# Gate and up weights of a feed-forward unpacked in the feed-forward itself, down weights alone in the rotary stage

## The chip, the cores and the metric

The kernel runs on one core of one Trainium2 chip. The metric is the device time of one execution in microseconds (us). The engines are TensorE (PE; its weight loads are PEld), VectorE (DVE), ScalarE (ACT), GpSimd (POOL) and SyncE (SP), which only issues DMAs here. Each engine runs its own queue in order; semaphores are the only thing that ties the queues together.

## What is computed

Two transformer-like layers over 16 batches of 64 tokens with 512 channels (1024 tokens). Layer 0 is a windowed attention and a base layer with routed low-rank experts. Layer 1 is an attention with 32 query heads, 8 key heads and rotary embedding, then a feed-forward with 4-bit weights (inner width 1376). Only the last matters for the change:

```python
def _dequant(qweight, scales, qzeros, g_idx):
    shifts = jnp.arange(PACK, dtype=jnp.uint32) * BITS            # 8 values of 4 bits in one word
    w = (qw[:, None, :] >> shifts[None, :, None] & MAXQ).reshape(-1, qweight.shape[1])
    z = ((qz[:, :, None] >> shifts[None, None, :] & MAXQ) + 1).reshape(qzeros.shape[0], -1)
    s = scales[g_idx]
    return (w.astype(scales.dtype) - z[g_idx].astype(scales.dtype)) * s
...
Wg = _dequant(gate_qweight, ...)   # 512 x 1376
Wu = _dequant(up_qweight, ...)     # 512 x 1376
Wd = _dequant(down_qweight, ...)   # 1376 x 512
# feed-forward: (silu(x @ Wg) * (x @ Wu)) @ Wd
```

Unpacking an element is thus shift and mask, minus zero point, times scale; zero point and scale are rows of a table chosen by `g_idx`.

## The kernel before

The program is a sequence of stages: `windowed_attention`, `routed_lora`, `rotary_attention`, `gate_up`, `down`. Between two stages all engines meet at a barrier. Matrix products are made by `three_passes` (L754 to L756): each float32 operand is split into a high part (by ScalarE) and a low part (high subtracted, by GpSimd for weights, by VectorE for activations), and high x high, low x high and high x low are summed.

`rotary_attention` handles the eight key heads in four pairs of two. A pair has 16 steps, a step being one tile of 128 tokens of one key head with its four query heads. In all there are 64 steps, numbered `n = step_number(b, c)` from 0. Every engine has its own function `step(b, c)`, written out by hand, and the order of its lines is the order of its queue; work of neighbouring tiles is interleaved in it. With j = n mod 4:

- TensorE: `turn` of tile n-2, `project` of one rotary unit, `project_out` of tile n-3 (L754 to L756 with `woh`/`wol` and `oh`/`ol`), `weighted` of n-2, a second `project`, the value projection if j = 2, `scores` of n+1 (L1578). `project_out` waits for `ol_ready`, from VectorE's `low_out`.
- VectorE: `low_out` of tile n-3 (L1465), `minimum` of n (L1444, L1449), `subtract_zeros` (L877), `rotary` (L1433 to L1435) for the first unit, `add` of n-3 (L1470), `probabilities` (L1455, L1459), `multiply_scales` (L886), `rotary` for the second unit, `unpack_weights` of the next unit of weights (L867). Rotary units are 0 and 1 in steps with j = 0, 2 and 3 with j = 1, 4 with j = 2, none with j = 3 (`ROTARY_OF`).
- GpSimd: `rotary_sum` for the same units (L1297, L1301), `low_piece` (L214) of a piece of the next head's projection weights when one is due (n mod 8 from 1 to 6, `PIECE_AT`; the key and value pieces are 128 x 512, the others 128 x 1024), then `gather_scales` (L858), an indirect DMA that brings scale and zero-point rows.
- SyncE: `load_piece` (L198), which waits in this same step for the `low_piece` whose buffer it reuses, `load_packed` (L850), `store_weights` (L899).

The 4-bit weights are unpacked in 43 of the 64 steps, one unit a step: `Q_UNITS` = 43 units, 32 of them "wide" (128 x 344 of gate or up) and 11 of "down" (128 x 512). Unit u is worked on in step u+1 and its rows are gathered two steps earlier into one of two buffers `sz`. The finished float32 weights are stored in HBM (`w_wide`, `w_down`).

`gate_up` first normalises the activations (`norm_rows`, `norm_turn`, `norm_high`, `norm_low`), then makes 11 tiles of the inner width. For each it loads one gate and one up tile of weights (`wf`, L1714, four buffers, two issues a tile pair), ScalarE makes `wh` (L1737), GpSimd `wl` (L1727), TensorE four products, ScalarE the tanh (L1749), and VectorE two operations for each half of the tokens (L1773, L1775). `down` multiplies by the down weights `wd`, which `gate_up` loads whole at its beginning.

Of the kernel before, what the change touches and what calls it, by code (L numbers as in the profile page):

```python
# [86 lines left out]
def build_program(nc, a, out):  # L87
    with ExitStack() as top:
# [24 lines left out]
        g["w_wide"] = nc.dram_tensor("w_wide", (2 * DC * P, INTER), F32).ap()  # L113
        g["w_down"] = nc.dram_tensor("w_down", (INTER, D), F32).ap()
        g["w_stored"] = [top.enter_context(nc.semaphore(f"w_stored{i}")) for i in range(2)]
# [714 lines left out]
def unit_shape(u):  # L830

    if u < WIDE_UNITS:
        return P, QCOLS
    return inner(u - WIDE_UNITS), D

def load_packed(sp, a, g, u):

    rows, cols = unit_shape(u)
    packed = P // PACK  # L840
    if u >= 2:
        sp.wait_ge(g["q_used"], u - 1)
    if u < WIDE_UNITS:
        chunk, q = u // QPIECES, u % QPIECES
        w = a[MATS[chunk // DC][0] + "_qweight"]
        src = bass.AP(w.tensor, w.offset + packed * (chunk % DC) * INTER + QCOLS * q, [[INTER, packed], [0, PACK], [1, cols]])
    else:
        w = a["down_qweight"]
        src = bass.AP(w.tensor, w.offset + packed * (u - WIDE_UNITS) * D, [[D, rows // PACK], [0, PACK], [1, cols]])
    sp.dma_start(g["qraw"][0:rows, u % 2, 0:cols], src).then_inc(g["q_landed"][u % 2], 16)  # L850

def gather_scales(pool, g, u):

    if u >= 2:
        pool.wait_ge(g["w_ready"], u - 1)
    table, width = (g["table_wide"], 2 * QCOLS) if u < WIDE_UNITS else (g["table_down"], 2 * D)
    pool.indirect_dma_start(g["sz"][:, u % 2, 0:width], None, table,  # L858
                            bass.IndirectOffsetOnAxis(ap=g["index"][:, u:u + 1], axis=0)).then_inc(g["sz_landed"][u % 2], 16)

def unpack_weights(dve, g, u):

    rows, cols = unit_shape(u)
    raw = g["qraw"][0:rows, u % 2, 0:cols]
    dve.wait_ge(g["q_landed"][u % 2], 16 * (u // 2 + 1))
    dve.tensor_scalar(raw, raw, g["nib"][0:rows, 0:1], 15, ALU.logical_shift_right, ALU.bitwise_and).then_inc(g["qn_ready"], 1)  # L867

def subtract_zeros(dve, g, u):  # L870

    rows, cols = unit_shape(u)
    dve.wait_ge(g["qn_ready"], u + 1)
    dve.wait_ge(g["sz_landed"][u % 2], 16 * (u // 2 + 1))
    if u >= 2:
        dve.wait_ge(g["w_stored"][u % 2], 16 * (u // 2))
    dve.tensor_tensor(g["dq"][0:rows, u % 2, 0:cols], g["qraw"][0:rows, u % 2, 0:cols], g["sz"][0:rows, u % 2, cols:2 * cols],  # L877
                      ALU.subtract).then_inc(g["q_used"], 1)

def multiply_scales(dve, g, u):

    rows, cols = unit_shape(u)
    w = g["dq"][0:rows, u % 2, 0:cols]
    dve.wait_ge(g["q_used"], u + 1)
    dve.tensor_tensor(w, w, g["sz"][0:rows, u % 2, 0:cols], ALU.mult).then_inc(g["w_ready"], 1)  # L886

def store_weights(sp, g, u):

    rows, cols = unit_shape(u)
    if u < WIDE_UNITS:
        chunk, q = u // QPIECES, u % QPIECES
        dst = g["w_wide"][chunk * P:chunk * P + rows, q * QCOLS:(q + 1) * QCOLS]
    else:
        r0 = (u - WIDE_UNITS) * P
        dst = g["w_down"][r0:r0 + rows, :]
    sp.wait_ge(g["w_ready"], u + 1)
    sp.dma_start(dst, g["dq"][0:rows, u % 2, 0:cols]).then_inc(g["w_stored"][u % 2], 16)  # L899
# [237 lines left out]
def rotary_attention(nc, a, g):  # L1137
# [37 lines left out]
    def unit_at(n):  # L1175

        return n - 1 if 1 <= n <= Q_UNITS else None
# [787 lines left out]
```

## Time and profile before

| | before |
|---|---|
| median of 3 timed runs | 1169.86 us (1169.71 to 1169.95) |
| the profiled execution's own time | 1171.48 us |
| its span in the profile | 1169.7 us |
| busy: PE, DVE, POOL, ACT | 1037.1, 796.0, 457.7, 349.8 us |
| rotary stage, first to last masked scores (L1444) | 363.5 to 951.8 us |
| start of the first load of `gate_up` | 976.0 us |

The span runs from the first to the last instruction that the profile shows. Every row of the trace gives start, duration, engine, line, operation and tiles; an idle time ahead of an instruction stands in brackets with the engine and line that ended it. L numbers are lines of the kernel before.

### The profile page before, as it was taken

The numbers are of one execution on the slowest core, as the hardware profiler recorded it, in microseconds if no ns is written. First come the engines' busy times: TensorE is split into PE (matmuls) and PEld (weight loads), VectorE is DVE, ScalarE is ACT, GpSimd is POOL, SyncE is SP.
The fourth block names the chain that finished last, engine by engine and source line by source line (L and its number), as shares of the span: only waits on it lengthen the run. The fifth ranks groups of instructions, "written<-read, shape, count | busy, mean of one in ns | idle before, by whom it ended". The sixth has DMA issues, their size and how long they took to land. (4 is left out here: it accounts for less than half of the span.)

```text
span 1169.7 us, 13349 instructions
## 1 busy us (share of the span) xinstructions
PE 1037.1 (89%) x4696; PEld 741.4 (63%) x4696; DVE 796.0 (68%) x1251; ACT 349.8 (30%) x926; POOL 457.7 (39%) x296
## 2 busy tenths in 40 slices
PE   5688877877878799999999999999999986999998
PEld 2333333344557567777777677677777765888787
DVE  4899998759566687778878888787676655222223
ACT  3232332213212332333333333333343332222131
POOL 3566655445515443444434434434243102222121
PEclk8899998869888899999999999999999998999999
DMA  7000000000311332332333325421010005211001
GB/s 258 1 1 0 1 1 1 1 18 1 104 50 52 118 123 78 127 112 88 109 100 118 126 80 168 161 97 45 27 46 18 1 2 168 53 38 32 1 1 72
DMA packets 60962, 75.91 MB, mean 65 GB/s; under 512 B 8444, under 2 KB 44068, under 8 KB 60888
## 3 DMA queue, kind: packets, MB, share of 16 engines
q1 hardware_dynamic: 56032, 57.66, 15.7%
q0 software_dynamic: 4144, 17.04, 4.5%
q8 instruction: 38, 0.62, 0.2%
q10 hardware_dynamic: 720, 0.36, 0.1%
q14 instruction: 28, 0.23, 0.1%
HBM read 64.37 MB, written 10.68 MB: 64 GB/s over the span
## 5 line engine op out<-in xcount | busy, mean ns | idle before, releaser
L1301 POOL TENSOR_TENSOR shared<-shared 128x512 f32<-128x512 f32 x64 | 83.7, 1307 | 201.6 <-DVE shared L1435 201.3
L754 PE MATMUL ps<-woh,oh 128*128 128x512 f32 x256 | 108.8, 425 | 32.9 <-DVE ol L1465 28.1
L1370 ACT ACTIVATE c_xn<-c_xn,c_mn 128x64 f32<-128x64 f32 x256 | 86.0, 337 | 155.6 <-DVE c_mn L1449 155.6
L754 PE MATMUL ps<-xh,wqh 128*128 128x512 f32 x256 | 106.6, 416 | 0.4 <-DVE shared L1435 0.4
L756 PE MATMUL ps<-woh,ol 128*128 128x512 f32 x256 | 104.7, 409 | 0.0
L755 PE MATMUL ps<-wol,oh 128*128 128x512 f32 x256 | 104.3, 408 | 0.0
L1433 DVE TENSOR_TENSOR shared<-ps,cs 128x512 f32<-128x512 f32 x80 | 54.9, 687 | 70.6 <-PE ps L756 70.6
L756 PE MATMUL ps<-xh,wql 128*128 128x512 f32 x256 | 100.4, 392 | 0.0
L755 PE MATMUL ps<-xl,wqh 128*128 128x512 f32 x256 | 99.9, 390 | 0.0
L540 DVE TENSOR_TENSOR r<-ps,vpad 128x512 f32<-128x512 f32 x128 | 79.4, 683 | 27.4 <-PE ps L629 27.4
L372 POOL TENSOR_TENSOR r<-r 128x1024 f32<-128x1024 f32 x32 | 77.1, 2410 | 50.4 <-DVE r L540 50.3
L1470 DVE SCALAR_TENSOR_TENSOR x<-ps,gate,x 128x512 f32<-128x512 f32 x64 | 48.0, 750 | 70.9 <-PE ps L756 70.2
L754 PEld LDWEIGHTS ps<-woh,oh 128*128 128x128 f32 x256 | 50.1, 196 | 54.1 <-DVE ol L1465 31.8
L1578 PEld LDWEIGHTS ps<-shared 128*128 128x128 f32 x512 | 66.3, 193 | 8.7 <-issue 5.2
L1383 ACT ACTIVATE oh<-ps 128x512 fp32r<-128x512 f32 x64 | 38.3, 598 | 104.8 <-PE ps L1603 104.8
L754 PE MATMUL ps<-xh,wh 128*128 128x512 f32 (+1 forms) x176 | 68.7, 390 | 1.0 <-POOL wl L1727 1.0
L1578 PE MATMUL ps<-shared 128*128 128x64 f32 x512 | 65.2, 271 | 3.8 <-POOL shared L1301 3.8
L756 PE MATMUL ps<-xh,wl 128*128 128x512 f32 (+1 forms) x176 | 68.6, 390 | 0.0
L755 PE MATMUL ps<-xl,wh 128*128 128x512 f32 (+1 forms) x176 | 68.5, 389 | 0.0
L1727 POOL TENSOR_TENSOR wl<-wf,wh 128x512 fp32r<-128x512 f32 (+1 forms) x22 | 28.6, 1318 | 82.9 <-ACT wh L1737 82.9
L629 PE MATMUL ps<-turned,spread 128*128 128x512 f32 x128 | 54.2, 506 | 7.4 <-DVE r L540 5.9
L754 PEld LDWEIGHTS ps<-xh,wqh 128*128 128x128 f32 x256 | 48.1, 188 | 18.2 <-issue 8.6
(172 smaller groups left out, 2387.8 us busy)
## 6 DMA issues: line engine op xcount, KB each, us to landing
stage<-in_wq SPq DMA_DIRECT2D x16, 512.0 KB, 4.1
stage<-in_wo SPq DMA_DIRECT2D x16, 512.0 KB, 3.8
w_wide<-dq SPq DMA_DIRECT2D x32, 172.0 KB, 4.9
wf<-w_wide SPq DMA_DIRECT2D x20, 256.0 KB, 3.4
qraw<-in_gate_qweight SPq DMA_DIRECT2D x16, 172.0 KB, 4.3
qraw<-in_up_qweight SPq DMA_DIRECT2D x16, 172.0 KB, 3.7
qraw<-in_down_qweight SPq DMA_DIRECT2D x10, 256.0 KB, 4.5
w_down<-dq SPq DMA_DIRECT2D x10, 256.0 KB, 6.0
```

The source lines that it names most:

```text
L372: pool.tensor_tensor(r2[:, 2 * m:2 * m + 2, :], r[:, w:w + 2, :], r[:, w + GW:w + GW + 2, :], ALU.add).then_inc(rsum_ready, 1)
L540: dve.tensor_tensor(r[:, w, :], RING[(2 + n) % 3], vpad[:, i % 3, w:w + D], ALU.mult)\
L629: pe.matmul(RING[(2 + n) % 3], spread[:, w % GW, :], turned[:, w // GW, :], start=True, stop=True)\
L754: pe.matmul(dst, lh, rh, start=(first and c == 0), stop=False)
L755: pe.matmul(dst, lh, rl, start=False, stop=False)
L756: last = pe.matmul(dst, ll, rh, start=False, stop=(final and c == chunks - 1))
L1301: pool.tensor_tensor(qT[:, h * TPH:(h + 1) * TPH, :, p - 1, :], turn(ra), turn(rb), ALU.add)\
L1370: act.activation(part, part, ACT.Exp, scale=-1.0, bias=mn[:, c % 2, u:u + 1], accum_out=sm[:, c % 2, u:u + 1]).then_inc(exp_ready, 1)
L1383: act.activation(by_batch(oh, c), weighted_sum, ACT.Copy).then_inc(oh_ready, 1)
L1433: dve.tensor_tensor(A, bank, cs[:, 0, :].unsqueeze(1).broadcast_to([P, nb, C]), ALU.mult)
L1470: dve.scalar_tensor_tensor(x[:, i, :], ps[:, WO[c % 2], :], gate[:, 1:2], x[:, i, :], ALU.mult, ALU.add)\
L1578: last = pe.matmul(dst[:, u * C:(u + 1) * C], qT[:, i, k, 2 * hp:2 * hp + 2, :].rearrange("p h t -> p (h t)"), kT[:, i * P + k * C:i * P + ...
```

## The change

Gate and up units are no longer unpacked in the rotary stage. There, for each of their 32 units, GpSimd gathers the scale and zero rows as before, and SyncE copies them from the buffer into a new tensor `sz_wide` in HBM. The 11 down units are still unpacked on VectorE, in steps with n mod 4 = 2 (n = 2, 6, ... 42). The wide fetches fill the other steps, from n = 3 to 44. `PLAN` maps a step to its fetch; a fetch is issued by GpSimd in the step before (`ahead`), and waits for the store (wide) or the multiplication (down) of the fetch two earlier, whose buffer it takes. `gate_up` now loads the packed words (four DMAs a tile) and the scale and zero rows (two DMAs) into three buffers, and VectorE unpacks each tile with three operations of 128 x 512, twice within the normalisation, twice behind it, then two tiles ahead of use.

```diff
+DOWN_AT = 2
+def fetch_plan():
+    plan, wide, down, n = {}, 0, 0, 2
+    while wide < WIDE_UNITS or down < NTI:
+        if n % TPH == DOWN_AT and down < NTI:
+            plan[n] = (len(plan), WIDE_UNITS + down)
+            down += 1
+        elif n % TPH != DOWN_AT and wide < WIDE_UNITS:
+            plan[n] = (len(plan), wide)
+            wide += 1
+        n += 1
+    return plan
+def fetch_done(eng, g, f):
+    u = next(unit for number, unit in PLAN.values() if number == f)
     if u < WIDE_UNITS:
...
+        same = [v for number, v in PLAN.values() if number <= f and number % 2 == f % 2 and v < WIDE_UNITS]
+        eng.wait_ge(g["sz_stored"][f % 2], 16 * len(same))
     else:
...
+        eng.wait_ge(g["wd_ready"], u - WIDE_UNITS + 1)
+def fetch_scales(pool, g, f, u):
+    if f >= 2:
+        fetch_done(pool, g, f - 2)
+    table = g["table_wide"] if u < WIDE_UNITS else g["table_down"]
+    pool.indirect_dma_start(g["sz"][:, f % 2, 0:width_of(u)], None, table,
+                            bass.IndirectOffsetOnAxis(ap=g["index"][:, u:u + 1], axis=0)).then_inc(g["sz_landed"][f % 2], 16)
+def store_scales(sp, g, f, u):
+    chunk, q = u // QPIECES, u % QPIECES
+    sp.wait_ge(g["sz_landed"][f % 2], 16 * (f // 2 + 1))
+    sp.dma_start(g["sz_wide"][chunk * P:(chunk + 1) * P, :, q * QCOLS:(q + 1) * QCOLS],
+                 g["sz"][:, f % 2, 0:2 * QCOLS].rearrange("p (e n) -> p e n", e=2)).then_inc(g["sz_stored"][f % 2], 16)
...
@@ SyncE, step @@
-                u = unit_at(n)
-                if u is not None:
-                    if 2 <= u + 2 < Q_UNITS:
-                        load_packed(sp, a, g, u + 2)
-                    store_weights(sp, g, u)
+                if n - 1 in PLAN:
+                    f, u = PLAN[n - 1]
+                    if u < WIDE_UNITS:
+                        store_scales(sp, g, f, u)
+                    else:
+                        store_down(sp, g, u - WIDE_UNITS)
+                if n in PLAN and WIDE_UNITS <= PLAN[n][1] < Q_UNITS - 2:
+                    load_down(sp, a, g, PLAN[n][1] - WIDE_UNITS + 2)
...
@@ GpSimd, step @@
-                u = unit_at(step_number(b, c))
-                if u is not None and u + 2 < Q_UNITS:
-                    gather_scales(pool, g, u + 2)
+                ahead = step_number(b, c) + 1
+                if ahead in PLAN:
+                    fetch_scales(pool, g, *PLAN[ahead])
...
@@ VectorE, step @@
-                u = unit_at(step_number(b, c))
-                if u is not None:
-                    subtract_zeros(dve, g, u)
+                f, u = PLAN.get(step_number(b, c), (0, 0))
+                t = u - WIDE_UNITS
+                if t >= 0:
+                    subtract_zeros(dve, g, f, t)
...
@@ gate_up @@
+        DEQUANT_AT = {3: 0, 5: 1}
...
+                if k >= 3:
+                    sp.wait_ge(w_ready, k - 2)
+                for c in range(DC):
+                    src = bass.AP(q.tensor, q.offset + packed * c * INTER + P * t, [[INTER, packed], [0, PACK], [1, w]])
+                    sp.dma_start(raw[:, k % 3, c * P:c * P + w], src).then_inc(landed[k % 3], 16)
+                rows = g["sz_wide"][m * DC * P:(m + 1) * DC * P, :, t * P:t * P + w].rearrange("(c p) e n -> p e c n", p=P)
+                for e in range(2):
+                    sp.dma_start(columns(sz[:, k % 3, e, :], k), rows[:, e, :, :]).then_inc(landed[k % 3], 16)
+                if k == 5:
...
+            for i in range(2, NT):
+                norm_rows(dve, g, n, xn, i)
+                norm_low(dve, g, n, XT, i - 2)
+                if i in DEQUANT_AT:
+                    dequantise(DEQUANT_AT[i])
+            norm_low(dve, g, n, XT, NT - 2)
+            norm_low(dve, g, n, XT, NT - 1)
+            dequantise(2)
+            dequantise(3)
             for t in range(NTI):
...
+                if t + 2 < NTI:
+                    unpack(2 * t + 4)
+                    subtract(2 * t + 4)
+                    unpack(2 * t + 5)
+                    scale(2 * t + 4)
+                    subtract(2 * t + 5)
+                    scale(2 * t + 5)
```

Three queues show what moved. GpSimd in steps 5 and 6: `shared` are the rotary sums, `wol` the split of an output piece, the DMA the gather. Before:

```order
L1301 TENSOR_TENSOR shared<-shared 128x8x64 [waits c_sc_done,c_rope_a] x2
L214 TENSOR_TENSOR wol<-stage,woh 128x1024 [waits high_ready]
L858 DMA sz<-table_wide,index 128x688 [waits c_w_ready]
L1301 TENSOR_TENSOR shared<-shared 128x8x64 [waits c_sc_done,c_rope_a]
L214 TENSOR_TENSOR wol<-stage,woh 128x1024 [waits high_ready]
```

and after the change:

```order
L1328 TENSOR_TENSOR shared<-shared 128x8x64 [waits c_sc_done,c_rope_a] x2
L215 TENSOR_TENSOR wol<-stage,woh 128x1024 [waits high_ready]
L876 DMA sz<-table_down,index 128x1024 [waits sz_stored0]
L1328 TENSOR_TENSOR shared<-shared 128x8x64 [waits c_sc_done,c_rope_a]
L215 TENSOR_TENSOR wol<-stage,woh 128x1024 [waits high_ready]
```

The gather stands in the same place behind the split. Before it fetched for step 7 and waited for VectorE's multiplication; now it fetches the down rows for step 6 and waits for a store.

SyncE in the same two steps (the first three rows are step 5, the others step 6), before:

```order
L198 DMA stage<-in_wk 128x4x128 [waits low_ready]
L850 DMA qraw<-in_gate_qweight 128x1x344 [waits c_q_used]
L899 DMA w_wide<-dq 128x344 [waits c_w_ready]
L198 DMA stage<-in_wq 128x4x256 [waits low_ready]
L850 DMA qraw<-in_gate_qweight 128x1x344 [waits c_q_used]
L899 DMA w_wide<-dq 128x344 [waits c_w_ready]
```

and after (the first two rows are step 5):

```order
L199 DMA stage<-in_wk 128x4x128 [waits low_ready]
L884 DMA sz_wide<-sz 256x1x344 [waits c_sz_landed0]
L199 DMA stage<-in_wq 128x4x256 [waits low_ready]
L884 DMA sz_wide<-sz 256x1x344 [waits c_sz_landed1]
L895 DMA qraw<-in_down_qweight 128x1x512 [waits c_q_used]
```

The store that signals `sz_stored0` stands behind the load of a weight piece, which waits for `low_ready`, the split of GpSimd's step 5.

VectorE at the beginning of step 6, after the change:

```order
L1490 TENSOR_TENSOR ol<-ps,oh 128x2x4x64 [waits c_oh_ready]
L1469 SCALAR_TENSOR_TENSOR c_xn<-ps,mask 128x256 [waits c_pr_ready,c_sc_done]
L1474 TENSOR_REDUCE c_mn<-c_xn 128x4 [waits c_masked]
L912 TENSOR_TENSOR dq<-qraw,sz 128x512 [waits w_stored0,c_sz_landed0,c_qn_ready]
L1458 TENSOR_TENSOR shared<-ps,cs 128x512 [waits c_rope_ready,c_proj_done]
```

The subtraction (L912, before L877) waits for the landing of that gather, and the rest of the step is queued behind it.

## Rows read from the trace of the kernel before

**Rows 1.** Page, busy time, share of the span and instructions
```profile
PE 1037.1 (89%) x4696; PEld 741.4 (63%) x4696; DVE 796.0 (68%) x1251; ACT 349.8 (30%) x926; POOL 457.7 (39%) x296
```

**Rows 2.** Timeline of DVE: masked scores of steps 4, 44, 48, 56
```profile
399.95 0.41 DVE L1444 SCALAR_TENSOR_TENSOR c_xn<-ps,mask 128x256 f32<-128x256 f32 x1
...
793.78 0.41 DVE L1444 SCALAR_TENSOR_TENSOR c_xn<-ps,mask 128x256 f32<-128x256 f32 x1
...
827.71 0.42 DVE L1444 SCALAR_TENSOR_TENSOR c_xn<-ps,mask 128x256 f32<-128x256 f32 x1
...
899.26 0.42 DVE L1444 SCALAR_TENSOR_TENSOR c_xn<-ps,mask 128x256 f32<-128x256 f32 x1
```

**Rows 3.** Timelines of POOL, steps 21 and 22, and of DVE
```profile
578.56 2.52 POOL L214 TENSOR_TENSOR wol<-stage,woh 128x1024 fp32r<-128x1024 f32 x1
581.21 1.08 POOL L858 DMA_INDIRECT sz<-table_wide,index  x1
...
580.10 1.35 DVE L877 TENSOR_TENSOR dq<-qraw,sz 128x344 f32<-128x344 int32 x1
```

**Rows 4.** Timelines of POOL, DVE and PE, steps 49 to 51, without unpacking
```profile
849.50 1.30 POOL L1301 TENSOR_TENSOR shared<-shared 128x512 f32<-128x512 f32 x1 [5.13 <-DVE shared L1435]
850.75 1.31 POOL L214 TENSOR_TENSOR wkvl<-stage,wkvh 128x512 fp32r<-128x512 f32 x1
...
850.50 0.42 DVE L1449 TENSOR_REDUCE c_mn<-c_xn 128x4 f32<-128x256 f32 x1
...
858.33 0.48 PE L754 MATMUL ps<-woh,oh 128*128 128x512 f32 x1
```

**Rows 5.** DMA issues, KB, us to landing: 785:790, 792:800, 765:772, 738:746
```profile
w_down<-dq SPq DMA_DIRECT2D x1, 256.0 KB, 3.3
...
w_down<-dq SPq DMA_DIRECT2D x1, 192.0 KB, 4.0
...
sz<-table_down,index POOLq DMA_INDIRECT x1, 4.2
...
w_down<-dq SPq DMA_DIRECT2D x2, 256.0 KB, 6.6
...
sz<-table_down,index POOLq DMA_INDIRECT x2, 7.0
```

**Rows 6.** Timeline of DVE, step 42: a down unit, to the end of `low_out`
```profile
778.49 0.72 DVE L877 TENSOR_TENSOR dq<-qraw,sz 128x512 f32<-128x512 int32 x1
...
782.79 2.92 DVE L886 TENSOR_TENSOR dq<-dq,sz 128x512 f32<-128x512 f32 x1
785.63 0.47 DVE L867 TENSOR_SCALAR qraw<-qraw,nib 96x512 int32<-96x512 int32 x1
786.02 0.68 DVE L1465 TENSOR_TENSOR ol<-ps,oh 128x512 fp32r<-128x512 f32 x1
```

**Rows 7.** PE after its longest gap; then windows, with PEclk before the last two
```profile
391.91 0.77 PE L754 MATMUL ps<-woh,oh 128*128 128x512 f32 x1 [6.08 <-DVE ol L1465]
...
396.00:398.00 2.00, 2.00 (x8) 1.06 (x6) 0.59 (x1) 0.00 (x0) 1.45 (x1) 0.52 0.00 0
398.00:400.00 2.00, 2.00 (x19) 1.75 (x16) 1.97 (x7) 1.20 (x3) 0.60 (x1) 1.00 0.54 169
```

**Rows 8.** Timelines of POOL and DVE: gather behind step 1's split, step 2's subtraction
```profile
384.95 0.97 POOL L858 DMA_INDIRECT sz<-table_wide,index  x1
...
382.81 0.82 DVE L877 TENSOR_TENSOR dq<-qraw,sz 128x344 f32<-128x344 int32 x1
```

**Rows 9.** `gate_up`: timelines of PE and DVE; DMA issues of 975:1030
```profile
984.36 0.47 PE L754 MATMUL ps<-xh,wh 128*128 128x512 f32 x1 [0.99 <-POOL wl L1727]
...
999.40 0.69 DVE L1773 SCALAR_TENSOR_TENSOR sg<-th,ps 128x512 f32<-128x512 f32 x1 [2.59 <-ACT th L1749]
...
1010.28 0.69 DVE L1773 SCALAR_TENSOR_TENSOR sg<-th,ps 128x512 f32<-128x512 f32 x1 [2.59 <-ACT th L1749]
...
wf<-w_wide SPq DMA_DIRECT2D x14, 256.0 KB, 3.7
```

More of the change, by code:

```diff
@@ L112, in build_program @@
         g["table_down"] = nc.dram_tensor("table_down", (GD, 2 * D), F32).ap()
-        g["w_wide"] = nc.dram_tensor("w_wide", (2 * DC * P, INTER), F32).ap()
+        g["sz_wide"] = nc.dram_tensor("sz_wide", (2 * DC * P, 2, INTER), F32).ap()
         g["w_down"] = nc.dram_tensor("w_down", (INTER, D), F32).ap()
+        g["sz_stored"] = [top.enter_context(nc.semaphore(f"sz_stored{i}")) for i in range(2)]
         g["w_stored"] = [top.enter_context(nc.semaphore(f"w_stored{i}")) for i in range(2)]
@@ L853, in gather_scales @@
[L853 to L867, printed above, removed]
@@ L870, in subtract_zeros @@
[L870 to L886, printed above, removed]
@@ new lines, with rows_of, width_of @@
+PLAN = fetch_plan()
+def rows_of(u):
+    return P if u < WIDE_UNITS else inner(u - WIDE_UNITS)
+def width_of(u):
+    return 2 * QCOLS if u < WIDE_UNITS else 2 * D
+def fetch_done(eng, g, f):
+    u = next(unit for number, unit in PLAN.values() if number == f)
+    if u < WIDE_UNITS:
+        same = [v for number, v in PLAN.values() if number <= f and number % 2 == f % 2 and v < WIDE_UNITS]
+        eng.wait_ge(g["sz_stored"][f % 2], 16 * len(same))
+    else:
+        eng.wait_ge(g["wd_ready"], u - WIDE_UNITS + 1)
@@ new lines, in load_down, with unpack_down @@
+def load_down(sp, a, g, t):
+    rows = inner(t)
+    if t >= 2:
+        sp.wait_ge(g["q_used"], t - 1)
+    w = a["down_qweight"]
+    src = bass.AP(w.tensor, w.offset + P // PACK * t * D, [[D, rows // PACK], [0, PACK], [1, D]])
+    sp.dma_start(g["qraw"][0:rows, t % 2, :], src).then_inc(g["q_landed"][t % 2], 16)
+def unpack_down(dve, g, t):
+    raw = g["qraw"][0:inner(t), t % 2, :]
+    dve.wait_ge(g["q_landed"][t % 2], 16 * (t // 2 + 1))
+    dve.tensor_scalar(raw, raw, g["nib"][0:inner(t), 0:1], 15, ALU.logical_shift_right, ALU.bitwise_and).then_inc(g["qn_ready"], 1)
@@ new lines, in subtract_zeros, with multiply_scales @@
+def subtract_zeros(dve, g, f, t):
+    w = inner(t)
+    dve.wait_ge(g["qn_ready"], t + 1)
+    dve.wait_ge(g["sz_landed"][f % 2], 16 * (f // 2 + 1))
+    if t >= 2:
+        dve.wait_ge(g["w_stored"][t % 2], 16 * (t // 2))
+    dve.tensor_tensor(g["dq"][0:w, t % 2, :], g["qraw"][0:w, t % 2, :], g["sz"][0:w, f % 2, D:2 * D], ALU.subtract)\
+       .then_inc(g["q_used"], 1)
+def multiply_scales(dve, g, f, t):
+    w = g["dq"][0:inner(t), t % 2, :]
+    dve.wait_ge(g["q_used"], t + 1)
+    dve.tensor_tensor(w, w, g["sz"][0:inner(t), f % 2, 0:D], ALU.mult).then_inc(g["wd_ready"], 1)
@@ L903, in routed_lora, with store_down @@
+def store_down(sp, g, t):
+    rows = inner(t)
+    sp.wait_ge(g["wd_ready"], t + 1)
+    sp.dma_start(g["w_down"][t * P:t * P + rows, :], g["dq"][0:rows, t % 2, :]).then_inc(g["w_stored"][t % 2], 16)
 def routed_lora(nc, a, g):
@@ L1200, in rotary_attention @@
         g["dq"] = sb("dq", [P, 2, D])
-        for name in ("qn_ready", "q_used", "w_ready"):
+        for name in ("qn_ready", "q_used", "wd_ready"):
             g[name] = sem(name)
@@ L1495, in step @@
                     probabilities(b, c)
-                if u is not None:
-                    multiply_scales(dve, g, u)
+                if t >= 0:
+                    multiply_scales(dve, g, f, t)
                 for p in units[1:]:
                     rotary(b, sl + 1, p)
-                if u is not None and u + 1 < Q_UNITS:
-                    unpack_weights(dve, g, u + 1)
+                if 0 <= t < NTI - 1:
+                    unpack_down(dve, g, t + 1)
             norm_rows(dve, g, n, xn, 0)
@@ L1514, in _ @@
                 rotary(0, 0, p)
-            unpack_weights(dve, g, 0)
+            unpack_down(dve, g, 0)
             for c in range(HEAD):
@@ L1684, in gate_up @@
         step = sem("step")
-        wf_landed = [sem(f"wf_landed{i}") for i in range(4)]
+        landed = [sem(f"landed{i}") for i in range(3)]
+        qn_ready = sem("qn_ready")
+        q_used = sem("q_used")
+        w_ready = sem("w_ready")
         wd_landed = sem("wd_landed")
```

78 lines of the change are left out of this document (36 added, 42 removed).

## The prediction, made before the changed kernel ran

> **What bounds the kernel now.** The page comes first: TensorE is busy for 89% of the span, more than any other engine [rows 1]. The change touches two stages, so the next view is the timeline, read by step of the rotary stage. A step n (0 to 63) is one pass of `step` on each engine; on VectorE it begins with the masked scores, L1444. Step 4 begins at 399.95 us and step 44 at 793.78: 393.83 us for forty steps, each with one unit of weights to unpack. Steps 48 to 56 have no unit and take 899.26 - 827.71 = 71.55 us for eight [rows 2]. In them TensorE has no gap. I call this the free rate. Forty steps at the free rate are 5 x 71.55 = 357.75 us, so all unpacking in this stretch costs 36.1 us today. It costs that much because VectorE does it between two things that TensorE waits for: `unpack_weights` stands ahead of `low_out`, whose result `project_out` needs.
>
> **What the change removes.** 32 of the 43 steps lose their three VectorE instructions. Taking the whole stretch at the free rate first, and pricing the steps that keep a down unit apart, removes 36.1 us.
>
> **What it adds in the rotary stage: a gather that is asked for too late.** Before, the gather for step n is issued in GpSimd's step n-2. Now it is issued as the last thing of GpSimd's step n-1. For a down unit n-1 is a step with two rotary sums, and the second of them needs the last VectorE work of that step. Before, in step 21, GpSimd's split of the weight piece runs from 578.56 to 581.08 and the gather behind it is issued at 581.21; VectorE's subtraction of step 22 begins at 580.10 [rows 3]. The gather that today serves a later step would, in the changed order, be the one this subtraction waits for. So it is late even if nothing else is.
>
> There is something else. The gather for step n first waits until the buffer two fetches back has been stored (`sz_stored0`). SyncE issues that store in its own step n-1, behind `load_piece`, and that load waits for the weight split of GpSimd's step n-1. So the chain is: last rotary sum, weight split, store issued and landed, gather issued and landed, subtraction. Nothing in it can overlap.
>
> I lay this chain over a free step (49 to 50), where no unpacking disturbs the times [rows 4]. The rotary sum runs 849.50 to 850.80. The split follows it: 1.31 us for the small piece (ends 852.06), 2.52 us for a large one [rows 3] (ends 853.3). Steps n with n mod 8 = 2 follow a small piece, those with n mod 8 = 6 a large one.
> - Store. Issue follows the split by about 0.1 us, behind the load's own 0.45. The nearest rows are a 256 KB store behind a 256 KB load, 3.3 us, and a 192 KB store behind a 512 KB load, 4.0 us [rows 5]. The new store has 344 KB, so I add 0.4 us to each, and 0.5 us more to the second, whose row was issued later behind its load. Behind a small load (large piece, n mod 8 = 6): 0.55 + 3.7 = 4.2 after the split, 857.5. Behind a large load (n mod 8 = 2): 0.55 + 4.9 = 5.4, also 857.5.
> - Gather. Alone on the queues, a down gather lands 4.2 us after its issue [rows 5]: 857.6 + 4.2 = 861.8, say 861.9.
> - VectorE then needs, from the subtraction to the end of `low_out`, 8.2 us: in step 42 it is 778.49 to 786.70, with the multiplication stretched to 2.92 us beside GpSimd's split, which follows in the same way here [rows 6]. So 870.1.
> - TensorE wants that result at 858.33 [rows 4]. It waits 11.8 us.
>
> **The clock.** After such a wait TensorE also restarts slowly. There is one gap of this kind in the stage already: 6.08 us before 391.91. The granted clock is 0.52 from 396 to 398 and 1.00 only from 398 [rows 7]: 6.1 us at 1.2 GHz instead of 2.4, so 3.0 us lost. A gap of 11.8 us is longer, and I charge 3.0 for each. The Trainium skill (TensorE: Matmul & The Clock Gate, Part 1) says that for modelling, the ramp penalty is under 1% of a typical kernel span. By that the clock term would be at most 11.7 us in all and the time 1273. The row here shows the loss after a single gap, and this kernel would have one per down unit.
>
> So each late unit costs 11.8 + 3.0 = 14.8 us. Ten of them (n = 6, 10, ... 42) cost 148.
>
> The eleventh, n = 2, has no store to wait for. The gather issued at that place before goes out at 384.95 [rows 8], about 2 us behind the start of the subtraction. With some 5 us to landing, VectorE resumes about 7 us later than today. The step before it loses 1.8 us of unpacking, and the clock is low there already. I take +5.
>
> For the transfers the Trainium skill (DMA: Bandwidth & Descriptors, Anatomy of one DMA) has a fixed 2.0 us plus the bytes at 436 GB/s. Estimated from that page, the store behind its load lands after 3.4 or 4.0 us and the gather after 3.2. The two stand on average 2 us below the chain above, which makes the sum about 20 us less, 1271. The rows of this trace are higher and are what I use.
>
> **What it adds in the feed-forward.** A pair of weight tiles lasts 10.88 us on TensorE (1010.28 - 999.40) [rows 9]. VectorE gains per pair two unpackings (0.47), two subtractions (0.72) and two multiplications (about the same when not beside GpSimd) [rows 6]: 3.8 us beside the four of 0.69 it has [rows 9], 6.6 of 10.88. If GpSimd's two subtractions of 1.3 us block it in full it is 9.2, still under. The weights are made two tiles ahead, so this hides. Loads: three times 256 KB a tile instead of one, each landing in 3.7 us [rows 9] and now in six issues. Two tiles every 10.88 us leave 5.4 for each, and a load with three times the packets should land in about 6 with three buffers in turn. It hides too; if it did not, it would cost 1 us a tile, 20 in all. What does not hide is the start. Today the first product begins at 984.36 [rows 9]. Now VectorE must wait in the middle of the normalisation for the six loads of tile 0 (last issue about 978.5, landed about 982) and put two sets of three operations (1.9 us each) ahead of the last rows. I count 3.7 us for the first and 1.9 for the second; about 5 us of it reaches TensorE.
>
> **Sum.** The span before is 1169.7 us, as is the median of the timed runs (1169.86), so I add to that. 1169.7 - 36.1 + 148 + 5 + 5 = 1291.6.
>
> **The rivals.**
> - Not slower: the gather is in time after all. If GpSimd runs far enough ahead of VectorE, the data lie there when the subtraction comes. Then a down unit costs only what VectorE's 8.2 us exceed the room: 850.9 + 8.2 - 858.3 = 0.8 us, eleven times, so 1169.7 - 36.1 + 9 + 5 = 1148. It decides at the landing: the gather may land up to about 850.9 in the clock of [rows 4]. Against it: the sum ahead of the gather needs VectorE's own rotary work and itself ends at 850.80. It could only hold if the wait order were another than the code has. Chance 0.03.
> - The store is not on the path (it lands while the split runs). Then only the gather's own lead counts: 853.3 or 852.1, plus 0.1 + 4.2, plus 8.2, against 858.3, on average 6.9 us, with the clock 9.9. Ten times is 99: 1242. For it speaks only that buffers alternate; against it, that the store stands behind a load that waits for the split. Chance 0.07.
> - The clock costs nothing, as it falls rarely: 1262. Chance 0.05.
> - The chain is dearer, since the transfers meet others: in a busy stretch the same store takes 6.6 and the gather 7.0 us [rows 5]. Most of that traffic is gone, but GpSimd's other gathers now wait for stores too, and could push its rotary sums, on which the scores depend. At 5 us more a unit: 1341. Half of it is as likely as the whole. Chance 0.11.
>
> **How the numbers follow.** The forecast has 0.74. Within it VectorE's part may be 2.2 us shorter (the multiplication takes 0.72 instead of 2.92 if it misses GpSimd's split), and store and gather together 1 us shorter or 2.5 longer (half of the busy stretch's surplus): 1260 to 1317. The range must reach towards the cheaper rivals and the dearer one: 1242 to 1335. A measurement of this kernel can tell about 0.2% from no change. Faster by more than that is the first rival, 0.03; within it 0.01, for a half-late gather that uses up the gain; slower 0.96.
>
> **What would show it.** In the profile after: ten gaps of about 12 us ahead of `project_out` in the steps after a down unit, put down to VectorE's `ol`; VectorE idle about 11 us ahead of the down subtraction, released by the landing of `sz<-table_down`; GpSimd idle ahead of the down gather, released by a store into `sz_wide`; low granted clock after each gap; 71.5 us per eight steps plus two stalls, so about 101. In the feed-forward the first product comes some 5 us later after the stage's start and a pair still takes 10.9 us. The prediction is wrong if the down gather is issued before the last rotary sum of its step, if the gaps are under 8 us, or if pairs in the feed-forward take over 11.5 us.

## The result, and the profile after

| | before | after |
|---|---|---|
| median of the timed runs | 1169.78 us (4 runs) | 1287.70 us (4 runs, 1286.35 to 1290.57) |
| ratio to before | | 1.101 (95% interval 1.099 to 1.103) |
| span of the profiled execution | 1169.7 us | 1285.7 us |
| mean granted clock of TensorE | 0.946 | 0.906 |

The changed kernel is 118 us slower; 1291.6 was forecast. The spans can be cut at the same events in both traces (a step begins with its masked scores, now L1469):

| stretch | before | after | difference | forecast |
|---|---|---|---|---|
| start to step 0 | 363.52 | 363.24 | -0.3 | 0 |
| steps 0 to 4 (the eleventh unit, n = 2) | 36.43 | 40.48 | +4.05 | +5 |
| steps 4 to 44 (ten down units) | 393.83 | 496.16 | +102.3 | +111.9 |
| steps 44 to 63 | 157.98 | 159.16 | +1.2 | 0 |
| step 63 to the start of `gate_up` | 24.20 | 24.22 | 0 | 0 |
| `gate_up` and `down` | 193.71 | 202.44 | +8.7 | +5 |

The page of after, busy times first, which answers to [rows 1]; then its costliest idle times (line, engine, out<-in, count | busy, mean ns | idle before, releaser):

```profile
PE 1047.8 (81%) x4696; PEld 752.9 (59%) x4696; DVE 772.8 (60%) x1221; ACT 350.9 (27%) x926; POOL 456.9 (36%) x296
...
L755 PE MATMUL ps<-woh,oh 128*128 128x512 f32 x256 | 113.3, 443 | 131.1 <-DVE ol L1490 74.2
...
L912 DVE TENSOR_TENSOR dq<-qraw,sz 128x512 f32<-128x512 int32 (+1 forms) x11 | 7.6, 692 | 117.6 <-DMA sz<-table_down,index 117.6
```

TensorE and VectorE do nearly the work of before, and both have more idle time. The two large idle times stand where the chain of the prediction puts them: ahead of the down subtraction (L912), ended by the landing of its gather, and ahead of `project_out`, ended by `low_out` (L1490). The second is more than half of the 131.1 us; the rest is put down to "issue", and stands in the same places.

The third wait of the chain is in the view of waits for the stretch 403 to 900 us (steps 4 to 44: waiting engine, tile and line, what ended it, us in total, times, longest):

```profile
POOL sz L876 <- DMA sz_wide<-sz: 126.1, 25, 5.8
...
DVE dq L912 <- DMA sz<-table_down,index: 110.2, 10, 11.7
```

GpSimd's 25 waits there are for fetches of both kinds. The ten ahead of a down gather last 4.1 to 5.7 us, 5.0 on average.

One unit from start to end, n = 26. Timelines of POOL, DVE and PE (start, us, engine, line, operation, idle time before in brackets):

```profile
671.85 1.29 POOL L1328 TENSOR_TENSOR shared<-shared 128x512 f32<-128x512 f32 x1 [5.13 <-DVE shared L1460]
673.10 1.30 POOL L215 TENSOR_TENSOR wkvl<-stage,wkvh 128x512 fp32r<-128x512 f32 x1
680.00 0.96 POOL L876 DMA_INDIRECT sz<-table_down,index  x1 [5.60 <-DMA sz_wide<-sz]
...
684.40 0.69 DVE L912 TENSOR_TENSOR dq<-qraw,sz 128x512 f32<-128x512 int32 x1 [11.12 <-DMA sz<-table_down,index]
688.65 2.82 DVE L920 TENSOR_TENSOR dq<-dq,sz 128x512 f32<-128x512 f32 x1
691.79 0.68 DVE L1490 TENSOR_TENSOR ol<-ps,oh 128x512 fp32r<-128x512 f32 x1
...
692.57 0.77 PE L755 MATMUL ps<-woh,oh 128*128 128x512 f32 x1 [11.63 <-issue]
...
693.98 0.63 PE L755 MATMUL ps<-woh,oh 128*128 128x512 f32 x1
694.41 0.63 PE L756 MATMUL ps<-wol,oh 128*128 128x512 f32 x1
```

and the two DMAs that SyncE issued behind that split (672 to 676 us; count, KB each, us to landing):

```profile
stage<-in_wq SPq DMA_DIRECT2D x1, 512.0 KB, 4.3
sz_wide<-sz SPq DMA_DIRECT2D x1, 344.0 KB, 4.9
```

Read it as a chain: the last rotary sum, the split, which ends at 674.40, the store behind the load (4.9 us), the gather at 680.00, landed 4.3 us later, the subtraction at 684.40, `low_out` at 691.79, TensorE at 692.57. Laid against [rows 4], each piece is there and they follow one another. The trace writes "issue" instead of VectorE for this gap, but it ends as `low_out` does.

Behind the gap the products follow each other every 0.43 us (693.98 to 694.41) instead of about 0.23. The windows of the same place (engines' busy time with counts, then PEclk, DMA share, GB/s) answer to [rows 7]:

```profile
690.00:692.00 2.00, 0.00 (x0) 0.00 (x0) 2.00 (x3) 0.00 (x0) 0.92 (x1) 0.50 0.00 1
694.00:696.00 2.00, 2.00 (x6) 1.61 (x5) 0.00 (x0) 1.67 (x6) 0.71 (x1) 0.50 0.51 167
696.00:698.00 2.00, 2.00 (x7) 1.06 (x6) 0.00 (x0) 0.00 (x0) 1.98 (x2) 0.51 0.44 135
698.00:700.00 2.00, 2.00 (x18) 1.67 (x18) 1.90 (x4) 1.17 (x2) 1.63 (x2) 1.00 0.25 70
```

TensorE had stood idle since 680.9. It is granted 1.2 GHz (0.50) in the last part of this gap and on to about 698, then 2.4 GHz.

### The profile page after: what moved, and what is told of

Read it like the earlier page. It is cut to its first block and busy times, and to the rows that moved or that the text cites. A ratio compares the mean times of both kernels' runs of the same rounds, so it can differ in the third digit from the quotient of the medians.

```text
span 1285.7 us, 13384 instructions
## 1 busy us (share of the span) xinstructions
PE 1047.8 (81%) x4696; PEld 752.9 (59%) x4696; DVE 772.8 (60%) x1221; ACT 350.9 (27%) x926; POOL 456.9 (36%) x296
## 5 line engine op out<-in xcount | busy, mean ns | idle before, releaser
L755 PE MATMUL ps<-woh,oh 128*128 128x512 f32 x256 | 113.3, 443 | 131.1 <-DVE ol L1490 74.2
L755 PEld LDWEIGHTS ps<-woh,oh 128*128 128x128 f32 x256 | 53.3, 208 | 146.9 <-issue 69.4
L756 PE MATMUL ps<-wol,oh 128*128 128x512 f32 x256 | 109.4, 427 | 0.0
L757 PE MATMUL ps<-woh,ol 128*128 128x512 f32 x256 | 109.2, 427 | 0.0
L541 DVE TENSOR_TENSOR r<-ps,vpad 128x512 f32<-128x512 f32 x128 | 79.4, 683 | 28.6 <-PE ps L630 28.6
L912 DVE TENSOR_TENSOR dq<-qraw,sz 128x512 f32<-128x512 int32 (+1 forms) x11 | 7.6, 692 | 117.6 <-DMA sz<-table_down,index 117.6
L1771 POOL TENSOR_TENSOR wl<-wf,wh 128x512 fp32r<-128x512 f32 (+1 forms) x22 | 31.6, 1453 | 88.6 <-ACT wh L1781 88.6
L757 PEld LDWEIGHTS ps<-woh,ol 128*128 128x128 f32 x256 | 53.5, 209 | 13.8
```

What stands on the lines that cost most here:

```text
L541: dve.tensor_tensor(r[:, w, :], RING[(2 + n) % 3], vpad[:, i % 3, w:w + D], ALU.mult)\
L755: pe.matmul(dst, lh, rh, start=(first and c == 0), stop=False)
L756: pe.matmul(dst, lh, rl, start=False, stop=False)
L757: last = pe.matmul(dst, ll, rh, start=False, stop=(final and c == chunks - 1))
L1771: pool.tensor_tensor(tile_view(wl, k), tile_view(wf, k), tile_view(wh, k).bitcast(F32), ALU.subtract)\
```

## The experiments

The traces show that the chain exists. They don't show that its parts cost what the table gives them: that the store's place behind a load matters, that the relief is 36 us once the chain is gone, and that the slow clock costs anything. Each of the following kernels takes one of these. Before ran beside them at 1168.48 us (e1 to e4) and 1168.88 us (e5 to e7).

### e1: the store ahead of the load

```diff
@@ SyncE, step @@
-                due = piece_due(c, last)
-                if due:
-                    piece, db, odd = due
-                    load_number(PIECES * (2 * (b + db) + odd) + piece + 2)
                 if n - 1 in PLAN:
                     f, u = PLAN[n - 1]
...
                         store_down(sp, g, u - WIDE_UNITS)
+                due = piece_due(c, last)
+                if due:
+                    piece, db, odd = due
+                    load_number(PIECES * (2 * (b + db) + odd) + piece + 2)
```

> The changed kernel with one edit: in SyncE's step the store of the scale rows stands ahead of the load of the weight piece, so it no longer waits for GpSimd's split. The down gather keeps its place behind rotary sum and split. Theory (a chain of sum, split, store, gather): only the store's share of the lateness goes. The gather is issued 0.1 us after the split (852.1 or 853.3 in the clock of the free step) and lands after 5 us beside the piece's load, so VectorE waits 7 us instead of 11, each of ten units is 4 us cheaper, and the time is about 1248 us; the low clock after each gap stays. Rival (the wait comes from the amount of traffic, which is unchanged): 1288 us.

Measured: 1254.64 us, ratio 1.074 (1.072 to 1.077), 33 us below the changed kernel. Steps 4 to 44 take 461.4 us instead of 496.2. Timelines of POOL, DVE and PE for n = 10, then the DMA issues of 470 to 484 us:

```profile
474.53 1.30 POOL L215 TENSOR_TENSOR wkvl<-stage,wkvh 128x512 fp32r<-128x512 f32 x1
475.98 0.96 POOL L876 DMA_INDIRECT sz<-table_down,index  x1
...
482.21 0.69 DVE L912 TENSOR_TENSOR dq<-qraw,sz 128x512 f32<-128x512 int32 x1 [7.50 <-DMA sz<-table_down,index]
...
490.37 0.76 PE L755 MATMUL ps<-woh,oh 128*128 128x512 f32 x1 [8.02 <-issue]
```

```profile
sz_wide<-sz SPq DMA_DIRECT2D x1, 344.0 KB, 6.4
sz<-table_down,index POOLq DMA_INDIRECT x1, 6.2
```

GpSimd's wait is gone: the gather goes out right behind the split. VectorE still waits 7.9 us on average and TensorE 8.3. The store's place was thus worth only 3.1 of 11.5 us a unit, less than the 5.0 that GpSimd had waited on average. The rest went back to the gather. It now leaves together with the load of the next weight piece and the next store, and lands after 6.2 us here, 6.0 on average, instead of 4.3. I had expected 5, and the time is 6.6 us above the 1248 expected.

### e2: the fetch first in the step

e1, and in GpSimd's step the fetch ahead of the rotary sums:

```diff
@@ GpSimd, step @@
                 sl, j = c // TPH, c % TPH
+                ahead = step_number(b, c) + 1
+                if ahead in PLAN:
+                    fetch_scales(pool, g, *PLAN[ahead])
                 if projecting(c, last):
...
-                ahead = step_number(b, c) + 1
-                if ahead in PLAN:
-                    fetch_scales(pool, g, *PLAN[ahead])
```

> As the store-first kernel, and GpSimd issues the gather as the first thing of its step, ahead of the rotary sums and the split. Theory: the down gather lands before the subtraction, VectorE's wait for it and TensorE's gaps of 11.5 us go, the granted clock stays at 1.00, and eight steps take 71.5 plus two times 0.8 us (VectorE's 8.2 us against the room) = about 73. Forty steps 366 instead of 496, the head 8 us less: 1288 - 131 - 8 = 1149 us. Rival (GpSimd's waits for stores now stand ahead of its rotary sums and delay them and the scores): 1170 to 1210 us, with TensorE waiting for the rotary sums instead.

Measured: 1145.79 us, ratio 0.980 (0.978 to 0.983) to before, and 142 us below the changed kernel. The same work in another order is faster than before. Timeline of DVE, masked scores of steps 4 and 44, which answer to [rows 2]:

```profile
396.43 0.42 DVE L1469 SCALAR_TENSOR_TENSOR c_xn<-ps,mask 128x256 f32<-128x256 f32 x1
...
756.48 0.42 DVE L1469 SCALAR_TENSOR_TENSOR c_xn<-ps,mask 128x256 f32<-128x256 f32 x1
```

and its groups of instructions, 400 to 900 us:

```profile
L755 PE MATMUL ps<-woh,oh 128*128 128x512 f32 x223 | 89.8, 403 | 1.0 <-DVE ol L1490 0.6
...
L912 DVE TENSOR_TENSOR dq<-qraw,sz 128x512 f32<-128x512 int32 (+1 forms) x10 | 19.2, 1916 | 3.9 <-DMA sz<-table_down,index 3.9
```

The forty steps take 360.06 us. At the free rate they would take 357.75, so ten down units on time cost 2.3 us together. The relief is thus there as a term of its own once the gather is in time; how large it is also depends on where the stretch is cut, which is taken up below. The rival does not show: GpSimd waits 5.3 to 5.7 us for a store ahead of five of the ten gathers, and the steps keep to the free rate all the same. The subtraction now lasts 1.92 us instead of 0.69, since it meets GpSimd's work, and that costs nothing here.

### e7: the fetch between the rotary sums and the split

e1, and the fetch one place up:

```diff
@@ GpSimd, step @@
                     for p in ROTARY_OF[j]:
                         rotary_sum(b, sl + 1, p)
+                ahead = step_number(b, c) + 1
+                if ahead in PLAN:
+                    fetch_scales(pool, g, *PLAN[ahead])
                 due = piece_due(c, last)
...
-                ahead = step_number(b, c) + 1
-                if ahead in PLAN:
-                    fetch_scales(pool, g, *PLAN[ahead])
```

> As the store-first kernel, with GpSimd's gather between its rotary sums and its split instead of behind the split. Theory (the lateness is the sum of what stands ahead of the gather): it is issued 1.3 or 2.5 us sooner, VectorE waits 6.0 instead of 7.9 us, TensorE's gaps are 6.4 instead of 8.3, the restart at half clock stays, and ten units give 19 us: 1235. Rival (the transfers' contention with the piece load sets the landing): VectorE's wait falls by more than 2 us, as the gather now runs before that load starts, 1228 or less.

Measured: 1214.89 us, ratio 1.038 (1.034 to 1.043). Timelines of POOL, DVE and PE for n = 10, then the DMA issues of 466 to 472 us:

```profile
466.74 0.96 POOL L876 DMA_INDIRECT sz<-table_down,index  x1
467.71 1.32 POOL L215 TENSOR_TENSOR wkvl<-stage,wkvh 128x512 fp32r<-128x512 f32 x1
...
471.19 0.69 DVE L912 TENSOR_TENSOR dq<-qraw,sz 128x512 f32<-128x512 int32 x1 [4.46 <-DMA sz<-table_down,index]
475.44 0.68 DVE L920 TENSOR_TENSOR dq<-dq,sz 128x512 f32<-128x512 f32 x1
476.04 2.98 DVE L902 TENSOR_SCALAR qraw<-qraw,nib 128x512 int32<-128x512 int32 x1
...
479.72 0.77 PE L755 MATMUL ps<-woh,oh 128*128 128x512 f32 x1 [5.34 <-POOL wql L215]
```

```profile
sz<-table_down,index POOLq DMA_INDIRECT x1, 4.4
```

One place in the queue is worth 40 us (1254.6 to 1214.9), 33 of them in steps 4 to 44. The theory had 1235; the rival, 1228 or less, is what came. The split that the gather no longer stands behind is 1.3 or 2.4 us, 1.9 on average. VectorE's mean wait falls by more, from 7.9 to 4.45 us: the gather now leaves ahead of the piece load and lands after 4.4 us instead of 6.0. TensorE's gap falls from 8.3 to 4.8 us. (The trace names the split of `wql` for the gap of n = 10, but that had ended at 478.73; `low_out` ends at 479.62.)

VectorE's multiplication is 2.1 us shorter as well, and yet the gap falls by no more than the wait does. The next split of GpSimd now meets `unpack_weights` (L902), which takes 2.98 us instead of 0.47: the stretch has moved from one instruction of this chain to another. In n = 34, where L902 takes 0.47 us, and n = 42, behind which nothing is unpacked, TensorE's gap is 2.6 and 2.7 us, against 5.1 to 5.5 in the other eight. With e1 and e2 this is a series in which only the places of the store and the gather move; the time follows them.

### e3: TensorE kept busy while it waits

The changed kernel, in which TensorE makes 40 further products ahead of its wait, into the bank that `project_out` then overwrites. They take no part in the result.

```diff
@@ TensorE, project_out @@
-                pe.wait_ge(ol_ready, m + 1)
                 if c >= 2:
                     pe.wait_ge(x_ready, m - 1)
+                if m % TPH == 0 and 4 <= m <= 40:
+                    for r in range(WARM):
+                        pe.matmul(ps[:, WO[c % 2], :], g["xh"][:, r % DC, 0:P], g["xh"][:, r % DC, 0:HALF], start=True, stop=True)
+                pe.wait_ge(ol_ready, m + 1)
```

> The changed kernel, with 40 extra 128 x 512 products ahead of TensorE's wait in the step after each of ten down units (their result is overwritten by the product that follows). They take 9.2 us of a gap of 11.5 that TensorE has there anyway. Theory (each gap costs a restart at half clock on top): the granted clock stays at 1.00, the first products after the gap follow each other at 0.23 instead of 0.43 us, and each unit is 2.3 us cheaper: 1265 us. Rival (the low clock costs nothing, as TensorE is not what limits then): 1288 us. If the extra products reach beyond the wait, it is slower instead.

Measured: 1270.99 us, ratio 1.087 (1.084 to 1.090), 16.7 us below the changed kernel, though it does 400 products more. Its profiled execution was the slowest of the four (1274.26 us, with the lowest mean clock, 0.943 against 0.946 to 0.949), so what is read from the trace is at the low end. There steps 4 to 44 are 13.8 us shorter. Windows of this kernel around the restart of n = 18, and the whole stretch; then its PE timeline:

```profile
590.00:592.00 2.00, 2.00 (x10) 1.59 (x9) 0.28 (x1) 1.68 (x9) 0.00 (x0) 1.00 1.00 319
...
400.00:880.00 480.00, 456.70 (x2197) 358.99 (x2196) 256.90 (x419) 131.24 (x446) 163.75 (x119) 0.98 0.29 92
```

```profile
589.55 0.50 PE L755 MATMUL ps<-woh,oh 128*128 128x512 f32 x1 [2.59 <-DVE ol L1491]
```

Windows of the changed kernel, the same restart and the same stretch:

```profile
593.00:595.00 2.00, 1.67 (x4) 1.41 (x5) 0.98 (x3) 0.95 (x6) 0.00 (x0) 0.50 0.90 295
595.00:597.00 2.00, 2.00 (x6) 1.52 (x6) 0.00 (x0) 1.43 (x5) 1.06 (x2) 0.50 0.37 126
...
400.00:880.00 480.00, 376.56 (x1785) 292.45 (x1784) 243.80 (x408) 129.45 (x439) 158.00 (x116) 0.89 0.28 90
```

TensorE goes on at 2.4 GHz: ten products in two microseconds against six. The granted clock over the stretch rises from 0.89 to 0.98. Per late unit 12.46 us are lost instead of 13.84. Nearly all of these 1.4 us stand in the pace of the products: the twelve of `project_out` took 1.95 us longer than at full pace in the changed kernel, on average of the ten units, and 0.66 here. It is not the whole of it: in four of the ten restarts the products still came every 0.43 us at first (in n = 34 only from the second product on), although the gaps ahead were of the same kind, 2.3 us on average. Why these four fell back the runs don't tell.

### e4: the first two tiles unpacked later

In the feed-forward the first product comes 15.1 us after the stage's start in the changed kernel (8.4 before). This kernel is e2 with both tiles unpacked two blocks of the normalisation later:

```diff
-        DEQUANT_AT = {3: 0, 5: 1}
+        DEQUANT_AT = {5: 0, 7: 1}
```

> As the fetch-first kernel, and in the feed-forward the first two tiles are unpacked two rows later within the normalisation (behind rows 5 and 7 instead of 3 and 5). Theory (VectorE stands 3.0 us idle there for the loads of tile 0 while rows of the normalisation are still to do): the first product begins 3 to 4 us earlier after the stage's start, and the time is 3 us below the fetch-first kernel, 1146 us. Rival (the second tile is then what the products wait for): no difference.

Measured: 1145.83 us, no difference from e2 (1145.79). Timeline of PE in this kernel, the first product and the first one of the second group:

```profile
950.72 0.77 PE L755 MATMUL ps<-xh,wh 128*128 128x512 f32 x1 [0.53 <-POOL wl L1771]
...
959.05 0.67 PE L755 MATMUL ps<-xh,wh 128*128 128x512 f32 x1 [2.54 <-POOL wl L1771]
```

The first product comes 3.7 us earlier, 11.2 us after the start, and then the second tile's weights are late. The second pair of tiles begins 29.4 us after the start, against 28.6 in e2, so nothing of the earlier start is left there. The two stages are still 0.5 us shorter than in e2, because a gap at the fourth pair is missing here, which e5 is about. To shift VectorE's work within the start gained nothing.

### e5: the load of the down weights two tiles later

e2, with the load of `wd` behind tile 7 instead of tile 5:

```diff
-                if k == 5:
+                if k == 7:
                     full = (NTI - 1) * P
```

> As the fetch-first kernel, but the whole down weights are loaded behind tile 7 of the feed-forward instead of tile 5. Theory: there the loads of tile 6 land late because they queue behind that transfer, VectorE stands 9 us idle for them, and TensorE waits 1.0 us for h at the fourth pair. With the transfer behind tile 7 that gap goes and the time falls by 1 us (1145), which only the trace can show. Rival (the transfer then holds up tiles 8 and 9 in the same way): the gap moves to the fifth pair.

Measured: 1143.64 us, ratio 0.979 (0.976 to 0.983), against 1145.79 for e2, which ran at another time; the intervals overlap. The traces are clearer than the times. PE in e2, the first product of the fourth pair of tiles (`t` = 3):

```profile
992.03 0.47 PE L755 MATMUL ps<-xh,wh 128*128 128x512 f32 x1 [0.95 <-DVE h L1859]
```

In e5 this gap is gone, and the two stages take 202.44 us instead of 203.70. VectorE waits as long as before, but later, where TensorE doesn't need it:

```profile
992.02 0.49 DVE L1816 TENSOR_SCALAR raw<-raw,nib 128x512 int32<-128x512 int32 x1 [8.81 <-DMA d_sz<-sz_wide]
```

So the gap was the load of `wd` in the queue ahead of the tile's rows. The two pairs around it take 1.2 us more than twice 10.88 in e2. With the same code of these stages it is 1.0 us in the changed kernel and 3.7 in e7, so the totals of the stages differ by more than e5 gains, and the evidence is the missing gap, not the total.

### e6: the first tiles' rows from a second queue

e5, with the scale and zero rows of tiles 0 and 1 issued by ScalarE's queue, so that SyncE has four issues for each of them instead of six (`load_rows` holds the two DMAs, `rows_stored` the wait for the stores of the rows):

```diff
@@ SyncE @@
-                for e in range(2):
-                    sp.dma_start(columns(sz[:, k % 3, e, :], k), rows[:, e, :, :]).then_inc(landed[k % 3], 16)
+                if k >= 2:
+                    load_rows(sp, k)
...
@@ ScalarE @@
+            rows_stored(act)
+            load_rows(act, 0)
+            load_rows(act, 1)
             for i in range(NT):
                 norm_high(act, g, n, XT, i)
```

> As the previous kernel, and ScalarE's queue issues the scale rows of the first two tiles, so SyncE has four issues for each instead of six. Theory (the first unpacking waits for six issues of 0.6 us in a row): tile 0 lands 1 to 1.5 us earlier, tile 1 2.5 us earlier, the first product comes 1.5 us sooner after the stage's start, and the time is about 1143. Rival (the landing itself, not the issue, is what takes the time, or ScalarE's own issues delay its first splits): no change.

Measured: 1143.98 us, no difference from e5 (1143.64). The DMA issues of 938 to 944 us, at the stage's start, in e6 and then in e5:

```profile
d_sz<-sz_wide ACTq DMA_DIRECT2D x4, 256.0 KB, 4.4
raw<-in_gate_qweight SPq DMA_DIRECT2D x4, 64.0 KB, 4.3
```

```profile
d_sz<-sz_wide SPq DMA_DIRECT2D x2, 256.0 KB, 3.5
raw<-in_gate_qweight SPq DMA_DIRECT2D x4, 64.0 KB, 2.3
```

More is issued in the same six microseconds (the rows of two tiles instead of one), and each load takes longer to land. VectorE's wait for tile 0 ends 7.3 us after the stage's start, against 7.0 in e5. The issues alone were not what held the start.

## Why the prediction was right, point by point

**The relief (-36.1).** Right in kind: e2 brought the stretch to within 2.3 us of the free rate with ten down units still in it. It is 1.9 us too large, by the place of the cut at step 44 (see "What was not foreseen"). The first rival, a gather in time, had 1148 us; e2 is such a kernel and takes 1145.8.

**The late gather (ten times 11.8).** Right in kind and nearly in size: TensorE's gap is 11.48 us on average, VectorE's wait 11.02 where the prediction had about 11. Its parts hold too, on average of the units: the store behind a 512 KB load landed after 4.8 us (4.9 assumed) and behind a 256 KB load after 3.65 (3.7), the gather after 4.3 (4.2), and the multiplication beside GpSimd took 2.83 us (2.92). The Trainium skill (DMA: Bandwidth & Descriptors, Anatomy of one DMA) has its figures for DMAs that GpSimd issues; by an estimate from them the gather would land after 3.2 us, and the store's own transfer, if they held for SyncE as well, after 2.8. The rows here are 4.3 and 3.65 to 4.8, and the gather beside a load in e1 6.0. The measurement decides. The rival without the store in the chain (1242) is answered by the 4.1 to 5.7 us that GpSimd waits in each of the ten units, and by e1, which is that kernel: 1254.6. It lies above 1242 because the rival kept the gather at 4.2 us. The dearer rival (1341) needed a store of 6.6 and a gather of 7.0 us; none of the ten took more than 5.0 and 4.5.

**The clock (ten times 3.0).** The mechanism is right, the term was too dear. A unit costs (496.16 - 357.75) / 10 = 13.84 us, of which 11.48 are the gap, so 2.36 are the rest. In the trace 7 to 12 products come at 0.43 us instead of 0.23, which makes 1.3 to 2.4 us, 1.95 on average. Another 0.2 is what a unit on time costs in e2, and the last 0.2 stays open. The 3.0 was half of the 6.1 us that [rows 7] have from the restart to the first window at full clock. Those windows are 2 us long, which is too coarse for this: in n = 26 twelve products, 692.57 to 697.8, came at the slow pace, and 12 x 0.2 = 2.4. The gap of before at 391.91 also has twelve slow products. The pace of the products themselves was the row to read, and one gap did not tell that half of the ten would recover sooner. e3 shows 1.4 of the 2.36 as due to the clock, with four restarts of ten still slow. The rival in which the clock costs nothing would have steps 4 to 44 at 472.6 us (357.75 + 114.8); 496.2 was measured. By the Trainium skill (TensorE: Matmul & The Clock Gate, Part 1), the ramp is under 1% of a typical span. Here 10 x 2.36 = 23.6 us is 1.8% of 1287.7, if all of it is put to the clock, and the 13.8 us that e3 removed are 1.1%; this kernel has a long gap per unit and isn't typical.

**The eleventh unit (+5).** 4.05 us. Its gather waits for no store, as stated.

**The feed-forward (+5).** The weakest term: 8.7 us. The step that was mis-sized is the start, where 5 us were to reach TensorE and 6.7 did. The loads of tile 0 were to be complete 6 us after the stage's start and were after 7.1, for the issues take 0.6 us each on SyncE and the last load, the sixth, went out at 1086.55 and landed 3.8 us later. Timeline of VectorE in the changed kernel, where the stage starts at 1083.26: the wait for tile 0, and the wait in front of tile 6:

```profile
1090.38 0.48 DVE L1816 TENSOR_SCALAR raw<-raw,nib 128x512 int32<-128x512 int32 x1 [2.99 <-DMA d_sz<-sz_wide]
...
1126.71 0.49 DVE L1816 TENSOR_SCALAR raw<-raw,nib 128x512 int32<-128x512 int32 x1 [8.87 <-DMA d_sz<-sz_wide]
```

and of PE, where [rows 9] had the first product at 0.47 us; here the next one follows after 0.6 us, the pace of the lower clock. Then the first products of the third and the fourth pair:

```profile
1098.33 0.78 PE L755 MATMUL ps<-xh,wh 128*128 128x512 f32 x1
1098.91 0.63 PE L756 MATMUL ps<-xl,wh 128*128 128x512 f32 x1
...
1121.81 0.39 PE L755 MATMUL ps<-xh,wh 128*128 128x512 f32 x1
...
1133.54 0.47 PE L755 MATMUL ps<-xh,wh 128*128 128x512 f32 x1 [0.69 <-DVE h L1859]
```

Two further things were missed. From its first product to the second pair TensorE needs 1.1 us more than before, which is the lower clock: the first seven products are spread over 2.6 us instead of 1.5. And the load of `wd` puts a gap of 0.69 ahead of the fourth pair, which with what follows costs 1.0 us: VectorE's wait of 8.87 us in front of tile 6 stands in the way of `h`. 6.7 + 1.1 + 1.0 = 8.8. The prediction had the loads hidden throughout. It was right for the pairs from the second on that don't meet `wd`, which last 10.88 us as before. The third lasts 11.73 us (1121.81 to 1133.54), so this pair is above the 11.5 us that the prediction gave as a sign of being wrong; the first pair, with the start in it, lasts 12.6 (11.5 before).

**What was not foreseen.** Steps 44 to 63 take 1.2 us more, all of it in step 44, which is 11.46 us long instead of 10.28. It is no work that was added, but the place of the cut. Timelines of VectorE at the first rotary operation of step 44, in the kernel before and in e2, where nothing is late:

```profile
794.92 0.69 DVE L1433 TENSOR_TENSOR shared<-ps,cs 128x512 f32<-128x512 f32 x1 [0.28 <-PE ps L756]
```

```profile
759.46 0.69 DVE L1458 TENSOR_TENSOR shared<-ps,cs 128x512 f32<-128x512 f32 x1 [2.10 <-PE ps L757]
```

In e2 step 44 takes 12.12 us, as step 48 does in every trace, and VectorE waits 2.10 us for TensorE in it. Before, VectorE comes late into the step from the unpacking of step 43 (7.15 us instead of the 5.10 of e2), waits 0.28 us, and the step is 1.84 us shorter. In the changed kernel the wait is 1.46 us and the step 0.66 us shorter than in e2. So the cut at step 44 counts 1.84 us too much for the forty steps of before, and 0.66 too much for those of the changed kernel, and as much too little for the steps behind them; the difference is the 1.2 us. Cut at step 48 instead, the relief is 427.76 - 5.5 x 71.55 = 34.2 us.

**The sum.** The errors are of both signs: -9.6 for the ten units, -1 for the eleventh, +3.7 for the feed-forward, +1.2 for the late steps, -0.3 ahead of step 0. Together they are the 5.9 us between 1291.6 and the span of 1285.7. That the total came within 4 us of the median (1287.7) owes something to this, and 2 us of it to a median that lies above the span.

## What to carry to other kernels

When a fetch is moved by one place in its queue, write out what it stands behind, and for the wait it carries, what the releasing instruction stands behind on its own queue. Here this was a split on GpSimd, and a store behind a load that waited for the same split: one order of the same work took 1288 us, another 1146, and the kernel before 1169. Price the two sides apart, the relief against a stretch that is free of the work, and each late unit as a chain of rows laid over a step of that stretch. Where a chain is broken open, look at what its transfer will meet: e1 gave back 1.7 us of each gain because the gather then left together with a load.

## What the runs showed of the hardware

- A 512 KB gather landed after 4.0 to 4.6 us when it was issued ahead of the piece load (e7) or after both load and store had landed (the changed kernel), and after 5.6 to 6.4 us when all left together (e1); the 344 KB store of the same moment took 6.4 instead of 4.9 us.
- TensorE restarted at 1.2 GHz after each of the long gaps, and with 40 products put ahead of the wait it went on at 2.4 GHz in six of ten cases. In the other four it fell back at gaps of the same kind. In e7 it restarted at 1.2 GHz after gaps of 5.1 to 5.5 us, and after two of 2.6 and 2.7 us it went on at 2.4 GHz, in one of them for its first two products only.
- Two queues that loaded at once took longer for each load (64 KB: 4.3 us instead of 2.3; 256 KB: 4.4 instead of 3.5), so that the first tile was complete no sooner.
- VectorE's subtraction of 128 x 512 took 0.69 us in the changed kernel and 1.92 in e2, where it met GpSimd's split, and the multiplication went the other way, from 2.83 to 0.68. In e7 it was `unpack_weights` that met the split, 2.98 us instead of 0.47.
